# A gated delta rule on one core: products stored position by position, and some of them formed on GpSimd

## The chip, the core and the metric

The kernel is one program on 1 of the 8 cores of a Trainium2 chip. The metric is the device time of one execution in microseconds (us), median of several runs.

## What is computed

Two transformer layers over 2 x 512 tokens of width 256, each an attention and a mixture of experts, joined by modulated layer norms and residual sums. The change lies in the attention of the second layer, a gated delta rule with 16 heads, keys of 8 and values of 16 numbers:

```python
q = _l2norm(q) * SCALE; k = _l2norm(k)
def step(S, inp):                      # one token of one head
    q_t, k_t, v_t, g_t, b_t = inp
    S = S * exp(g_t)
    mem = einsum('bhk,bhkv->bhv', k_t, S)
    delta = (v_t - mem) * b_t
    S = S + einsum('bhk,bhv->bhkv', k_t, delta)
    return S, einsum('bhk,bhkv->bhv', q_t, S)
```

Its output goes through an RMS norm and a gate to the output projection. All of this is fp32.

## The kernel before, in words

Every partition holds one quarter (128 tokens, `CT`) of the tokens of one head of one batch. These are cut into `CC` = 16 chunks of `C` = 8 positions. Inside a chunk the recurrence is solved in closed form, and a scan over the 64 chunks of a sequence (`NB`) then carries the 8x16 state. Most operands are stored `(d c t)`: dimension, chunk, and the position inside the chunk innermost. A pair product is stored `(d c j)`, with the earlier position j innermost.

A sum over j, or over key dimensions, is done by TensorE: each product slice is the moving operand against the identity, and the slices add up in PSUM. An fp32 matmul stands in the trace as two MATMUL records, each of which streams all its columns. The stages, in order, with the lines of the profile:

- **Front** (VectorE, lines 1849 to 1958; GpSimd 643 to 662). Decays and betas, unit keys and queries (`unit`), the pair products k.k and q.k (`pair_products`, L1897; summed by TensorE at L1334), the rows `X24` = (16 value rows, 8 key rows) times beta (L1919, L1920), and the backward substitution (`rank_one` L1934, `less` L1939). GpSimd forms the decays `Di`, the scaled keys (L657) and the scaled queries `qa` (L661).
- **Value and matrix sums.** For each of 8 key dimensions k, VectorE multiplies all 24 rows of X24 by one row of R16 (L1970, 3072 elements). TensorE sums the 16 value rows over j, 8 slices of 256 columns (L1342). VectorE reduces the 8 key rows over j itself into the transition matrix `Msb` (L1980) and works on the query rows of the substitution between (L1934, L1939). There are three product buffers, so product k waits for TensorE's sum k-2 from the fourth on.
- **Query sums.** TensorE spreads the first two blocks of `Msb` (L1355). VectorE forms the query rows' key products `q_prod(t)` (L1995), TensorE adds them to `qa` (L1372, L1374), ScalarE copies the result to `Qp` (L917).
- **Output sums.** VectorE forms the query rows' value products `o_prod(t)` (L2002), (t+1) x 256 elements for position t; TensorE sums them (L1383), 36 slices of 256 columns. Ahead of them TensorE spreads the first half of the queries of group 0 (L1379), behind them the second half (L1387), which ScalarE copies (L936) ahead of `n_slot(2)` (L928), and the scan needs `n_slot(2)` for its ninth step.
- **Scan and states.** VectorE runs 63 steps of two products (L2020, one operand in PSUM) and two reductions (L2027). For every 8 steps (h = 0 to 7) `spread_m(h)` brings in a block of the matrix, GpSimd forms queries times states in 4 instructions (L674), TensorE sums them (L1400, 8 slices of 256 columns), and ScalarE copies them to `seqU` (L942). After every second h TensorE spreads them over the partitions and adds them to the output sums (L1409, 16 matmuls of 128 columns). `queries(g)` (L1362) brings in the queries of the next group.
- **Output.** Copies to `oT1`, norm, gate, projection, then the second mixture of experts, which starts when all of this is done.

Each engine runs its instructions in the order written; waits are on counting semaphores written out by hand. The loops of TensorE around the change, at L1381 and L1390, are

```python
for t in O_ORDER:
    pe.wait_ge(s["x_prod"], 2 * DK + O_ORDER.index(t) + 1)
    for j in range(t + 1):
        ins = pe.matmul(..., ident[:, :], o_prod(t)[:, :, :, j], ...)
...
for h in range(NHALF):
    if h + 2 < NHALF:
        spread_m(h + 2)
    if h % 2 == 0 and g + 1 < NCG:
        queries(g + 1)
    pe.wait_ge(s["state_prod"], h + 1)
```

## Time and profile before

| | before |
|---|---|
| median of 3 runs | 954.7 us (953.11 to 954.99) |
| profiled execution | 956.23 us |
| its span in the trace | 954.1 us |
| TensorE matmul busy | 862.5 us, 90% |
| VectorE busy | 538.6 us, 56% |
| GpSimd busy | 210.1 us, 22% |
| mean granted clock of TensorE | 0.951 |

The profiled execution is 2.1 us longer than its span, and 1.5 us longer than the median. Busy shares are over the whole program; the stages of the delta rule named above lie between 440 and 700 us.

### The profile page before, as it was taken

How to read it: one execution, taken by the hardware profiler on the slowest of the kernel's cores; microseconds unless marked ns; L12 is line 12 of the kernel's file. 1: busy time of each engine (PE TensorE's matmuls, PEld its weight loads, DVE VectorE, ACT ScalarE, POOL GpSimd, SP SyncE). 2: the span in 40 equal slices, each digit the busy share in tenths (PEclk: the TensorE clock that was granted, in tenths of full speed). 3: DMA queues.
4: the chain of work that ended last, by engine and by line, in shares of the span. 5: the costliest groups of instructions: out<-in, count | busy, mean ns of one | idle time of the engine just before them, and what ended most of it. 6: DMA issues, size and time to landing. Idle time of an engine off the chain costs nothing.

```text
span 954.1 us, 11526 instructions
## 1 busy us (share of the span) xinstructions
PE 862.5 (90%) x3978; PEld 588.0 (62%) x4008; DVE 538.6 (56%) x1275; ACT 253.9 (27%) x409; POOL 210.1 (22%) x189
## 2 busy tenths in 40 slices
PE   5889999879999999989869999899986799999983
PEld 4322333657777777754544475477753598999973
DVE  4787982654444444468999633387147533333426
ACT  2445775423333333335300000111121000000000
POOL 3630000212222222202200000255100243444410
PEclk9988999879999999999989999999997899999995
DMA  8763001101111111303300030000001589999944
GB/s 279 179 153 68 2 3 34 34 17 33 49 49 46 37 49 49 117 1 99 100 0 0 1 89 0 0 1 1 0 1 45 217 293 322 346 339 339 343 140 159
DMA packets 37122, 96.22 MB, mean 101 GB/s; under 512 B 4990, under 2 KB 17846, under 8 KB 36118
## 3 DMA queue, kind: packets, MB, share of 16 engines
q1 hardware_dynamic: 32982, 85.29, 27.9%
q0 software_dynamic: 3648, 9.97, 2.9%
q10 hardware_dynamic: 448, 0.39, 0.2%
q8 instruction: 26, 0.43, 0.2%
q14 instruction: 18, 0.15, 0.0%
HBM read 83.26 MB, written 13.16 MB: 101 GB/s over the span
## 4 chain that ended last, share of the span: by engine, by line
PE 78%; DVE 13%; DMA 4%; ACT 2%; issue 2%; SPq 1%; ACTq 0%; POOL 0%; DVEq 0%; POOLq 0%
PE psum L1225 15%; PE psum L1496 8%; PE psum L1506 7%; PE psum L1236 7%; PE psum L1342 6%; PE psum L1383 3%; PE psum L1409 3%; PE psum L1400 3%; PE psum L1104 3%; PE psum L1114 3%; PE psum L1125 3%; PE psum L1304 3%; PE psum L1374 2%; DVE small L1657 2%; PE psum L1314 1%
## 5 line engine op out<-in xcount | busy, mean ns | idle before, releaser
L1225 PE MATMUL psum<-xr,wr 128*128 128x512 f32 x600 | 158.9, 415 | 1.1 <-DVE arena L1806 1.1
L1225 PEld LDWEIGHTS psum<-xr,wr 128*128 128x128 f32 x600 | 116.0, 194 | 25.5 <-issue 1.4
L629 POOL TENSOR_TENSOR wr<-ring,wr 128x512 fp32r<-128x512 f32 (+1 forms) x50 | 54.5, 1109 | 196.6 <-ACT wr L797 196.6
L1657 DVE TENSOR_REDUCE small<-psum 128x1 f32<-128x512 f32 x128 | 81.0, 684 | 13.6 <-PE psum L1104 12.9
L1496 PEld LDWEIGHTS psum<-arena 128*128 128x128 f32 x700 | 83.3, 191 | 4.7 <-issue 1.5
L1496 PE MATMUL psum<-arena 128*128 128x128 f32 x700 | 84.0, 274 | 2.1 <-ACT arena L992 1.1
L1506 PE MATMUL psum<-arena 128*128 128x256 f32 x350 | 83.0, 384 | 1.9 <-DVE arena L2186 1.9
L1236 PE MATMUL psum<-hr,wr 128*128 128x512 f32 x300 | 76.2, 390 | 0.2 <-DVE hr L1744 0.2
L2175 DVE TENSOR_SCALAR arena<-psum,arena 128x256 f32<-128x256 f32 x35 | 16.9, 484 | 103.9 <-PE psum L1506 103.9
L674 POOL TENSOR_TENSOR arena<-hT,arena 128x512 f32<-128x512 f32 x32 | 36.2, 1163 | 165.1 <-ACT hT L936 140.3
L1769 DVE TENSOR_TENSOR hid<-hid,psum 128x512 f32<-128x512 f32 x50 | 34.4, 689 | 67.4 <-ACT hid L803 67.4
L776 ACT ACTIVATE arena<-psum 128x1024 f32<-128x1024 f32 x64 | 63.1, 1023 | 31.3 <-PE psum L1114 30.6
L1506 PEld LDWEIGHTS psum<-arena 128*128 128x128 f32 x350 | 64.3, 192 | 10.2 <-issue 2.3
L1342 PE MATMUL psum<-arena,ident 128*128 128x256 f32 x128 | 59.4, 642 | 9.4 <-DVE arena L1970 9.4
L1236 PEld LDWEIGHTS psum<-hr,wr 128*128 128x128 f32 x300 | 56.5, 189 | 12.4 <-issue 0.6
L691 POOL DMA_INDIRECT z_scratch<-arena x35 | 34.6, 989 | 97.7 <-DVE arena L2175 97.7
L810 ACT ACTIVATE hr<-hid 128x512 fp32r<-128x512 f32 x50 | 31.6, 632 | 90.7 <-DVE hid L1816 77.2
L1744 DVE TENSOR_TENSOR hr<-hid,hr 128x512 fp32r<-128x512 f32 x50 | 34.6, 692 | 35.5 <-ACT hr L810 35.4
L685 POOL DMA_INDIRECT arena<-h_scratch,arena x35 | 34.5, 987 | 86.0 <-DVE arena L2152 75.6
L1342 PEld LDWEIGHTS psum<-arena,ident 128*128 128x128 f32 x128 | 28.0, 219 | 40.5 <-issue 29.8
L992 ACT ACTIVATE arena<-psum 128x256 f32<-128x256 f32 x35 | 13.4, 384 | 145.0 <-PE psum L1485 145.0
L2186 DVE TENSOR_SCALAR arena<-psum,arena 128x128 f32<-128x128 f32 x175 | 48.2, 342 | 5.8 <-PE psum L1496 5.8
(360 smaller groups left out, 1276.1 us busy)
## 6 DMA issues: line engine op xcount, KB each, us to landing
arena<-in_w1u SPq DMA_DIRECT2D x35, 642.5 KB, 5.8
arena<-in_w1d SPq DMA_DIRECT2D x35, 640.0 KB, 5.3
ring<-in_w SPq DMA_DIRECT2D x25, 384.0 KB, 3.0
part_scratch<-arena SPq DMA_DIRECT2D x12, 256.0 KB, 4.2
arena<-z_scratch SPq DMA_DIRECT2D x8, 384.0 KB, 6.7
arena<-part_scratch SPq DMA_DIRECT2D x9, 256.0 KB, 7.8
qkv_scratch<-arena SPq DMA_DIRECT2D x4, 512.0 KB, 2.7
arena<-qkv_scratch SPq DMA_DIRECT2D x4, 512.0 KB, 4.0
```

The source lines that it names most:

```text
L629: pool.tensor_tensor(wr0[:, k, LO, part], ring0[:, k, part], wr0[:, k, HI, part], ALU.subtract).then_inc(s["w0_lo"], 1)
L674: ins = pool.tensor_tensor(sprod[:, h % 2, :, v, :].rearrange("p k (c t) -> p k c t", t=C), qB[g % 2][:, :, at8].rearrange("p k (c t) -> p ...
L691: pool.indirect_dma_start(z_dram, bass.IndirectOffsetOnAxis(ap=dst_i[:, r:r + 1], axis=0), yb[:, r % 3, :], None).then_inc(s[f"y_out{r % 3 ...
L776: act.activation(pexp[:, lo:lo + 2, :], psum[:, 2 + p % 2 * 2:4 + p % 2 * 2, :], ACT.Exp, scale=HD ** -0.5).then_inc(s["exp"], 1)
L1225: ins = pe.matmul(bank[2 * b + m][:, :], wr0[:, k, w, lo:lo + P], xr[:, x, f, half(b)], start=(f == 0 and (w, x) == PARTS[0]), stop=(f == ...
L1236: ins = pe.matmul(bank[4 + 2 * m + b][:, :], wr0[:, k, w, lo:lo + P], hr[:, b, x, :], start=(first and (w, x) == PARTS[0]), stop=(last and ...
L1342: ins = pe.matmul(bank[2 + k // 2][:, k % 2 * DV * CC:(k % 2 + 1) * DV * CC], ident[:, :], mn[k % 3][:, 0:DV, :].rearrange("p x (c j) -> p ...
L1496: ins = pe.matmul(bank[2 + r % 2 * 3 + k // 2][:, tile(k % 2)], wup1[:, r % 3, lo:lo + P], xgT[:, r % 2, f, :], start=(f == 0), stop=(f == ...
L1506: ins = pe.matmul(bank[1][:, 0:D], hact[:, r % 2, tile(k)], wdn1[:, r % 3, k * D:(k + 1) * D], start=(k == 0), stop=(k == NC1 - 1))
L1657: dve.tensor_reduce(nm[:, g % 2, at16:at16 + 1], full("scores", n), AX, ALU.max, negate=True).then_inc(s["bank_free"], 1)
L1744: dve.tensor_tensor(hr[:, b, LO, :], hid[:, 2 + b, :], hr[:, b, HI, :], ALU.subtract).then_inc(s[f"{name}_lo"], 1)
L2186: ins = dve.tensor_scalar(hact[:, r % 2, tile(k)], bank[2 + r % 2 * 3 + k // 2][:, tile(k % 2)], bias, 0.0, ALU.add, ALU.max)
```

## The change

The position in the chunk moves outermost and the chunk innermost in all the operands that are multiplied and summed: `(d t c)` for keys and queries, `(j x c)` for X24 and its products, `(j d c)` for the pair products, and `(g t v c)` for `seqU`. `unit` writes its result in the new order, from the old one; so do the rows of v, the decays and beta. The matmuls read slices without a stride. The reduction into `Msb` becomes three additions of halves. The eight `o_prod` move from VectorE to GpSimd, ahead of its state products. `spread_m(2)` moves from the loop over h to a place ahead of the last but one output sum. Half of the state products of the last block move from GpSimd to VectorE. Cut to what differs:

```diff
         QPROD = arena[:, 0:DK * PAIRS]
 
-        mn = [t.rearrange("p (x n) -> p x n", x=XR)
+        mn = [t.rearrange("p (j x c) -> p j x c", j=C, x=XR)
               for t in (arena[:, 0:XR * CT], arena[:, XR * CT:2 * XR * CT], KPROD[:, 0:XR * CT])]
         Nsb = arena[:, end:end + DV * CT]
...
+            return x.rearrange("p (j d c) -> p j d c", d=DV, c=CC)
 
         pa = KPROD[:, 0:2304].rearrange("p (u n v k x) -> p u n v k x", u=2, n=4, v=VV, k=DK)
         oT1 = KPROD[:, 0:DV * CT].rearrange("p (v n) -> p v n", v=DV)
         xn_flat = xn.rearrange("p t d -> p (t d)")
...
+        def turned(x, d):
+
+            return x.rearrange("p (d t c) -> p d t c", d=d, t=C)
...
 
-        X3 = X24.rearrange("p (d n) -> p d n", d=XR)
-        Xu = units(X24, XR)
-        R3 = R16.rearrange("p (d n) -> p d n", d=2 * C)
-        Ru = units(R16, 2 * C)
-        v3 = v2.rearrange("p (d n) -> p d n", d=DV)
+        Xt = X24.rearrange("p (j d c) -> p j d c", j=C, d=XR)
+        Ru = turned(R16, 2 * C)
 
         osq = hT.rearrange("p k (v n) -> p (k v) n", n=CT)
 
+        def state_product(eng, h, v):
+
+            at8 = slice(h % 2 * 64, h % 2 * 64 + 64)
+            return eng.tensor_tensor(sprod[:, h % 2, :, v, :].rearrange("p k (c t) -> p k c t", t=C),
+                                     qB[h // 2 % 2][:, :, at8].rearrange("p k (c t) -> p k c t", t=C),
+                                     Sall[:, 8 * h * VV * DK:8 * (h + 1) * VV * DK]
+                                     .rearrange("p (c v k) -> p v k c", v=VV, k=DK)[:, v]
+                                     .unsqueeze(3).broadcast_to((P, DK, 8, C)), ALU.mult)
+
         O_ORDER = (0, 1, 2, 3, 4, 5, 7, 6)
 
         def q_prod(i):
 
...
-            pool.tensor_tensor(qa.rearrange("p (d n) -> p d n", d=DK), q2.rearrange("p (d n) -> p d n", d=DK),
-                               by_dim(A0, DK), ALU.mult).then_inc(s["decays"], 1)
+            pool.tensor_tensor(qa.rearrange("p (t d c) -> p d t c", t=C, d=DK), qu,
+                               by_step(A0).unsqueeze(1).broadcast_to((P, DK, C, CC)),
+                               ALU.mult).then_inc(s["decays"], 1)
+
+            pool.wait_ge(s["x_prod"], 2 * DK)
+            pool.wait_ge(s["n_sum"], DK)
+            for t in O_ORDER:
+                if t == 6:
+                    pool.wait_ge(s["n_sum"], DK + 2)
+                pool.tensor_tensor(o_prod(t), Xt[:, 0:t + 1, 0:DV, :],
+                                   Ru[:, t, 0:t + 1, :].unsqueeze(2).broadcast_to((P, t + 1, DV, CC)),
+                                   ALU.mult).then_inc(s["out_prod"], 1)
+            pool.wait_ge(s["out_prod"], C)
 
...
                 pool.wait_ge(s["scan_hi"], 2 * (n0 + 7))
-                at8 = slice(h % 2 * 64, h % 2 * 64 + 64)
-                for v in range(VV):
-                    ins = pool.tensor_tensor(
-                        sprod[:, h % 2, :, v, :].rearrange("p k (c t) -> p k c t", t=C),
-                        qB[g % 2][:, :, at8].rearrange("p k (c t) -> p k c t", t=C),
-                        Sall[:, n0 * VV * DK:(n0 + 8) * VV * DK]
-                        .rearrange("p (c v k) -> p v k c", v=VV, k=DK)[:, v]
-                        .unsqueeze(3).broadcast_to((P, DK, 8, C)), ALU.mult)
-                ins.then_inc(s["state_prod"], 1)
+                for v in range(VV if h < NHALF - 1 else hv):
+                    ins = state_product(pool, h, v)
+                ins.then_inc(s["out_prod"], 1)
...
-                act.activation(seqU[:, :, h * 64:(h + 1) * 64],
-                               bank[5][:, h % 2 * 256:(h % 2 + 1) * 256].rearrange("p (v n) -> p v n", v=VV),
-                               ACT.Copy).then_inc(s["state_out"], 1)
+                act.activation(seqU[:, h // 2, :, :, h % 2 * 8:h % 2 * 8 + 8].rearrange("p t v c -> p v c t"),
+                               bank[5][:, h % 2 * 256:(h % 2 + 1) * 256]
+                               .rearrange("p (v c t) -> p v c t", v=VV, t=C), ACT.Copy).then_inc(s["state_out"], 1)
...
                     ins = pe.matmul(bank[2 + k // 2][:, k % 2 * DV * CC:(k % 2 + 1) * DV * CC], ident[:, :],
-                                    mn[k % 3][:, 0:DV, :].rearrange("p x (c j) -> p (x c) j", j=C)[:, :, j],
+                                    mn[k % 3][:, j, 0:DV, :].rearrange("p x c -> p (x c)"),
                                     start=(j == 0), stop=(j == C - 1), skip_group_check=True)
                 ins.then_inc(s["n_sum"], 1)
...
             for t in range(C):
                 pe.wait_ge(s["x_prod"], DK + t + 1)
                 to = bank[4 + t // 4][:, t % 4 * CT:(t % 4 + 1) * CT]
-                pe.matmul(to, ident[:, :], units(qa, DK)[:, :, :, t], start=True, stop=False, skip_group_check=True)
+                pe.matmul(to, ident[:, :], qa[:, t * CT:(t + 1) * CT], start=True, stop=False, skip_group_check=True)
                 for j in range(t + 1):
-                    ins = pe.matmul(to, ident[:, :], q_prod(t)[:, :, :, j], start=False, stop=(j == t),
+                    ins = pe.matmul(to, ident[:, :], q_prod(t)[:, j].rearrange("p x c -> p (x c)"), start=False, stop=(j == t),
                                     skip_group_check=True)
                 if t % 4 == 3:
                     ins.then_inc(s["n_sum"], 1)
             pe.wait_ge(s["qp_in"], 2)
             pe.matmul(bank[4][:, :], selg[:, 0, :], Qp[:, 0:4 * CT], start=True, stop=True).then_inc(s["queries"], 1)
             for t in O_ORDER:
-                pe.wait_ge(s["x_prod"], 2 * DK + O_ORDER.index(t) + 1)
+                if t == O_ORDER[-2]:
+                    spread_m(2)
+                pe.wait_ge(s["out_prod"], O_ORDER.index(t) + 1)
                 for j in range(t + 1):
                     ins = pe.matmul(bank[t // 2][:, t % 2 * 256:(t % 2 + 1) * 256], ident[:, :],
-                                    o_prod(t)[:, :, :, j],
+                                    o_prod(t)[:, j].rearrange("p x c -> p (x c)"),
                                     start=(j == 0 and t in O_ORDER[::2]), stop=False, skip_group_check=True)
...
             for h in range(NHALF):
                 g = h // 2
-                if h + 2 < NHALF:
+                if 0 < h < NHALF - 2:
                     spread_m(h + 2)
                 if h % 2 == 0 and g + 1 < NCG:
                     queries(g + 1)
-                pe.wait_ge(s["state_prod"], h + 1)
+                pe.wait_ge(s["out_prod"], C + (h + 1 if h < NHALF - 1 else NHALF + 1))
                 if h:
                     pe.wait_ge(s["state_out"], h)
...
-                            seqU[:, :, g * CT:(g + 1) * CT].rearrange("p v (c t) -> p t v c", t=C)[:, 2 * n:2 * n + 2],
+                            seqU[:, g, 2 * n:2 * n + 2].rearrange("p t v c -> p (t v c)"),
...
-            ch.link(dve.tensor_scalar(g_(0), ab2[:, 0, :], cols[:, DLT + 1:DLT + 2], None, ALU.add))
+            ch.link(dve.tensor_scalar(by_step(g_(0)), from_tokens(ab2[:, 0, :]), cols[:, DLT + 1:DLT + 2], None, ALU.add))
...
-            def unit(n, t):
-
-                t3 = t.rearrange("p (d n) -> p d n", d=DK)
+            def unit(n, t, to):
+
                 dve.wait_ge(s["d_act"], n + 7)
                 ch.link(dve.reciprocal(g_(8 + n), g_(8 + n)))
                 if n:
                     ch.link(dve.tensor_scalar(g_(9), g_(9), DK ** -0.5, None, ALU.mult))
-                dve.tensor_tensor(t3, t3, by_dim(g_(8 + n), DK), ALU.mult).then_inc(s["unit"], 1)
-
-            unit(0, k2)
+                dve.tensor_tensor(to, t.rearrange("p (d c t) -> p d t c", d=DK, t=C),
+                                  by_step(g_(8 + n)).unsqueeze(1).broadcast_to((P, DK, C, CC)),
+                                  ALU.mult).then_inc(s["unit"], 1)
+
+            unit(0, k2, ku)
...
                     for i in part:
-                        ins = dve.tensor_tensor(blocks(prod, i), ku[:, :, :, 0:i + 1],
-                                                left[:, :, :, i].unsqueeze(3).broadcast_to((P, DK, CC, i + 1)),
+                        ins = dve.tensor_tensor(blocks(prod, i), ku[:, :, 0:i + 1, :],
+                                                left[:, :, i, :].unsqueeze(2).broadcast_to((P, DK, i + 1, CC)),
                                                 ALU.mult)
...
-            t0, t1 = g_(0), g_(1)
-            first = [x.rearrange("p (c t) -> p c t", t=C)[:, :, 0] for x in (t0, t1, dec)]
-            dve.tensor_copy(t0, dec)
+            t0, t1, t2 = g_(0), g_(1), g_(7)
+            first = [x.rearrange("p (c t) -> p c t", t=C)[:, :, 0] for x in (t0, t1)]
+            dve.tensor_copy(from_tokens(t0), dec3)
             ch.link(dve.memset(t1, 0.0))
             dve.memset(first[0], 0.0)
-            ch.link(dve.tensor_copy(first[1], first[2]))
-            dve.tensor_tensor_scan(A0, t0, t1, 0.0, ALU.mult, ALU.add).then_inc(s["blocks"], 1)
-            unit(1, q2)
+            ch.link(dve.tensor_copy(first[1], dec3[:, 0, :]))
+            ch.link(dve.tensor_tensor_scan(t2, t0, t1, 0.0, ALU.mult, ALU.add))
+            dve.tensor_copy(by_step(A0), from_tokens(t2)).then_inc(s["blocks"], 1)
+            unit(1, q2, qu)
...
-            dve.tensor_tensor(X3[:, DV:XR, :], k2.rearrange("p (d n) -> p d n", d=DK), by_dim(t0, DK), ALU.mult)
-            x_rows = ch.mark(dve.tensor_tensor(X3[:, 0:DV, :], v3, by_dim(beta, DV), ALU.mult))
+            dve.tensor_tensor(Xt[:, :, DV:XR, :].rearrange("p j d c -> p d j c"), ku,
+                              by_step(t0).unsqueeze(1).broadcast_to((P, DK, C, CC)), ALU.mult)
+            x_rows = ch.mark(dve.tensor_tensor(Xt[:, :, 0:DV, :],
+                                               v2.rearrange("p (d c t) -> p t d c", d=DV, t=C),
+                                               by_step(beta).unsqueeze(2).broadcast_to((P, C, DV, CC)), ALU.mult))
...
-                prod = Sall[:, at:at + n * CC * i].rearrange("p (r c j) -> p r c j", r=n, c=CC)
-                return prod, dve.tensor_tensor(prod, Ru[:, part, :, i].unsqueeze(3).broadcast_to((P, n, CC, i)),
-                                               pair_row(Lr, i)[:, :, 0:i].unsqueeze(1).broadcast_to((P, n, CC, i)),
+                prod = Sall[:, at:at + n * CC * i].rearrange("p (r j c) -> p r j c", r=n, c=CC)
+                return prod, dve.tensor_tensor(prod, Ru[:, part, i, :].unsqueeze(2).broadcast_to((P, n, i, CC)),
+                                               pair_row(Lr, i)[:, 0:i, :].unsqueeze(1).broadcast_to((P, n, i, CC)),
                                                ALU.mult)
 
             def less(i, part, prod):
-                return dve.tensor_tensor(Ru[:, part, :, 0:i], Ru[:, part, :, 0:i], prod, ALU.subtract)
+                return dve.tensor_tensor(Ru[:, part, 0:i, :], Ru[:, part, 0:i, :], prod, ALU.subtract)
...
-                ins = dve.tensor_tensor(Ru[:, i, :, 0:i + 1],
+                ins = dve.tensor_tensor(Ru[:, i, 0:i + 1, :],
                                         bank[7 if i >= C - 2 else 6][:, lo:lo + CC * (i + 1)]
-                                        .rearrange("p (c j) -> p c j", c=CC), pair_row(Di, i), ALU.mult)
+                                        .rearrange("p (j c) -> p j c", c=CC), pair_row(Di, i), ALU.mult)
...
             for k in range(DK):
                 if k >= 3:
                     dve.wait_ge(s["n_sum"], k - 2)
-                made = dve.tensor_tensor(mn[k % 3], X3, R3[:, C + k, :].unsqueeze(1).broadcast_to((P, XR, CT)),
-                                         ALU.mult)
-                made.then_inc(s["x_prod"], 1)
+                prods = mn[k % 3]
+                dve.tensor_tensor(prods, Xt, Ru[:, C + k].unsqueeze(2).broadcast_to((P, C, XR, CC)),
+                                  ALU.mult).then_inc(s["x_prod"], 1)
 
                 i = C - 1 - k
                 if i:
-                    ch.need(turned)
+                    ch.need(solved)
                     prod, ins = rank_one(i, slice(i, C), 1024)
                     formed = ch.mark(ins)
                 dve.wait_ge(s["x_prod"], k + 1)
-                ins = dve.tensor_reduce(M3[:, k], units(mn[k % 3].rearrange("p x n -> p (x n)"), XR)[:, DV:XR],
-                                        AX, ALU.add)
-                reduced = ch.mark(ins)
+                ch.link(dve.tensor_tensor(prods[:, 0:4, DV:XR, :], prods[:, 0:4, DV:XR, :], prods[:, 4:8, DV:XR, :],
+                                          ALU.add))
+                halved = ch.mark(dve.tensor_tensor(prods[:, 0:2, DV:XR, :], prods[:, 0:2, DV:XR, :],
+                                                   prods[:, 2:4, DV:XR, :], ALU.add))
                 if i:
                     ch.need(formed)
-                    turned = ch.mark(less(i, slice(i, C), prod))
-                ch.need(reduced)
+                    solved = ch.mark(less(i, slice(i, C), prod))
+                ch.need(halved)
+                summed = ch.mark(dve.tensor_tensor(M3[:, k], prods[:, 0, DV:XR, :], prods[:, 1, DV:XR, :], ALU.add))
+            ch.need(summed)
             diag = Msb.rearrange("p (c e) -> p c e", c=CC)[:, :, 0:DK * DK:DK + 1]
-            dve.tensor_tensor(diag, diag, A0.rearrange("p (c t) -> p c t", t=C)[:, :, C - 1].unsqueeze(2)
+            dve.tensor_tensor(diag, diag, by_step(A0)[:, C - 1, :].unsqueeze(2)
                               .broadcast_to((P, CC, DK)), ALU.add).then_inc(s["m_done"], 1)
             dve.memset(Sall[:, 0:VV * DK], 0.0).then_inc(s["blocks"], 1)
 
-            ch.need(turned)
+            ch.need(solved)
...
             for t in range(C):
-                dve.tensor_tensor(q_prod(t), Xu[:, DV:XR, :, 0:t + 1],
-                                  Ru[:, t, :, 0:t + 1].unsqueeze(1).broadcast_to((P, DK, CC, t + 1)),
+                dve.tensor_tensor(q_prod(t), Xt[:, 0:t + 1, DV:XR, :],
+                                  Ru[:, t, 0:t + 1, :].unsqueeze(2).broadcast_to((P, t + 1, DK, CC)),
                                   ALU.mult).then_inc(s["x_prod"], 1)
-            dve.wait_ge(s["n_sum"], DK)
-            for t in O_ORDER:
-                if t == 6:
-                    dve.wait_ge(s["n_sum"], DK + 2)
-                dve.tensor_tensor(o_prod(t), Xu[:, 0:DV, :, 0:t + 1],
-                                  Ru[:, t, :, 0:t + 1].unsqueeze(1).broadcast_to((P, DV, CC, t + 1)),
-                                  ALU.mult).then_inc(s["x_prod"], 1)
-
...
             dve.wait_ge(s["scan_lo"], 2 * (NB - 1))
             dve.wait_ge(s["scan_hi"], 2 * (NB - 1))
+            dve.wait_ge(s["qB"], 2 * NCG)
+            dve.wait_ge(s["state_sum"], NHALF - 2)
+            dve.wait_ge(s["out_prod"], C + NHALF - 1)
+            for v in range(hv, VV):
+                ins = state_product(dve, NHALF - 1, v)
+            ins.then_inc(s["out_prod"], 1)
```

Here `turned(x, d)` is `(d t c)`, `from_tokens(x)` reads `(c t)` as t, c, and `by_step(x)` is `(t c)`.

## Rows read from the trace of the kernel before

**Rows 1.** Chain of waits, 440 to 700 us: start, duration, engine and line, pieces.

```profile
496.07 59.38 PE psum L1342 x128
...
557.18 0.46 PE psum L1372 x2
557.64 0.22 PE psum L1374 x2
...
560.74 1.81 PE psum L1374 x8
...
572.69 3.74 PE psum L1374 x16
...
577.61 2.08 PE psum L1379 x2
579.69 31.21 PE psum L1383 x72
...
639.04 3.45 PE psum L1400 x16
...
647.28 7.69 PE psum L1409 x32
```

**Rows 2.** Timeline of VectorE: start, duration, line, shape, idle before.

```profile
470.44 7.13 DVE L1897 TENSOR_TENSOR arena<-arena 128x1024 f32<-128x1024 f32 x8 [0.71 <-DMA arena<-qkv_scratch]
...
492.66 3.36 DVE L1970 TENSOR_TENSOR arena<-arena 128x3072 f32<-128x3072 f32 x1
...
500.97 1.21 DVE L1980 TENSOR_REDUCE arena<-arena 128x128 f32<-128x1024 f32 x1
502.10 0.35 DVE L1939 TENSOR_TENSOR arena<-arena 128x192 f32<-128x192 f32 x1
502.37 3.35 DVE L1970 TENSOR_TENSOR arena<-arena 128x3072 f32<-128x3072 f32 x1
...
507.40 3.35 DVE L1970 TENSOR_TENSOR arena<-arena 128x3072 f32<-128x3072 f32 x1
...
526.07 3.36 DVE L1970 TENSOR_TENSOR arena<-arena 128x3072 f32<-128x3072 f32 x1 [2.35 <-PE psum L1342]
...
613.18 0.47 DVE L2020 TENSOR_TENSOR arena<-arena,psum 128x128 f32<-128x128 f32 x2
...
613.99 0.48 DVE L2020 TENSOR_TENSOR arena<-arena,psum 128x128 f32<-128x128 f32 x2
```

**Rows 3.** Groups by shape on VectorE, 540 to 547 us (mean ns last).

```profile
L1995 DVE TENSOR_TENSOR arena<-arena 128x512 f32<-128x512 f32 x1 | 0.7, 684 | 0.0
...
L1995 DVE TENSOR_TENSOR arena<-arena 128x128 f32<-128x128 f32 x1 | 0.4, 387 | 2.3 <-PE psum L1342 2.3
```

**Rows 4.** Groups by shape on VectorE, 481.9 to 492.6 us.

```profile
L1939 DVE TENSOR_TENSOR arena<-arena 128x128 f32<-128x128 f32 x2 | 0.5, 284 | 0.0
```

**Rows 5.** Groups by shape on VectorE, 457.5 to 466.4 us.

```profile
L1897 DVE TENSOR_TENSOR arena<-arena 128x1024 f32<-128x1024 f32 x1 | 3.3, 3253 | 0.0
L1887 DVE TENSOR_TENSOR arena<-arena,rt 128x1024 f32<-128x1024 f32 x1 | 1.2, 1225 | 0.0
```

**Rows 6.** Timeline of GpSimd, 440 to 700 us.

```profile
457.68 3.32 POOL L657 TENSOR_TENSOR arena<-arena 128x1024 f32<-128x1024 f32 x1 [4.54 <-DVE arena L1887]
...
618.29 4.51 POOL L674 TENSOR_TENSOR arena<-hT,arena 128x512 f32<-128x512 f32 x4 [1.33 <-DVE arena L2027]
```

**Rows 7.** Groups by shape on ScalarE, 440 to 700 us.

```profile
L912 ACT ACTIVATE arena<-psum 128x256 f32<-128x256 f32 x8 | 4.4, 664 | 81.3 <-PE psum L1342 81.3
...
L942 ACT ACTIVATE hid<-psum 128x256 f32<-128x256 f32 x8 | 3.1, 384 | 31.7 <-PE psum L1400 31.7
```

**Rows 8.** Stretches: length; PE, PEld, DVE, ACT, POOL busy; clock; DMA share, GB/s.

```profile
464.00:466.00 2.00, 1.11 (x5) 1.11 (x6) 2.00 (x4) 0.84 (x2) 0.00 (x0) 0.60 0.77 294
470.00:472.00 2.00, 1.12 (x5) 1.06 (x6) 1.56 (x1) 0.83 (x2) 2.00 (x1) 1.00 0.14 44
...
577.00:578.00 1.00, 0.39 (x1) 0.39 (x2) 1.00 (x1) 1.00 (x3) 0.00 (x0) 0.52 0.00 0
```

34 lines of the change are left out of this document (19 added, 15 removed).

## The prediction

> **What bounds the kernel now.** The page's busy shares don't say what the delta rule waits for, so I read the chain of waits between 440 and 700 us first. From 496.07 on it is nearly all TensorE: the value sums (59.38 us), the query sums (to 576.43), the output sums (31.21 us), then eight state sums of 3.45 us and four spreads of 7.69 us [rows 1]. Next come the widths. A state sum reads 256 adjacent columns and takes 3.45/16 = 0.216 us a record. A value sum, also 256 columns against the same identity, reads every eighth word and takes 59.38/128 = 0.464 us; an output sum takes 31.21/72 = 0.433 us. The query sums show that the stride is the cause. All are 128 columns, and the stride in words is t+1: 0.22/2 = 0.11 us at t=0, 1.81/8 = 0.226 at t=3, 3.74/16 = 0.234 at t=7 [rows 1]. The spread (stride 8, 128 columns) takes 7.69/32 = 0.240. So from a stride of four words a record costs twice as much.
> The Trainium skill (SBUF — State Buffer, the note on cachelines in its DMA port part) says that SBUF is read in lines of 16 bytes and that an access pattern which leaves the line at every element is slower; the step to 0.226 us at 16 bytes agrees.
>
> VectorE is the second engine. In the value stage its round takes 5.03 us (502.37 to 507.40) against TensorE's 7.4, and from the sixth product on it waits about 2.35 us a round [rows 2]. Before 492.66 VectorE has no wait but one of 0.71 us for v's transfer, and sets the pace.
>
> **Front (VectorE, adds).** `unit` twice and the rows of v now read or turn every eighth word: 1024 + 1024 + 2048 elements. The price per element: a product of 128 with both inputs at stride 8 took 387 ns [rows 3], one of 128 with adjacent runs 284 ns [rows 4], so 0.8 ns more. Upper bound 4096 x 0.8 = 3.3 us; the lower is 0, since only one input of the three is strided. I take 0.65 ns, 2.7 us, near the upper end, plus 0.6 us for the short strided operations on 128 numbers and the new copy of A0. The wait for v's transfer, 0.71 us [rows 2], disappears behind that; the few products of one position that were strided gain 0.2 us. Net +2.4, rounded to +2.9 for semaphores (bounds 0 and +4).
> The Trainium skill (Vector Engine (DVE) Microarchitecture Reference, the part on the SBUF access granule) gives 2.5 ns a column where both sources or the output step by 24 words, against 1.05 adjacent; by that the three would cost an estimated 6 us and the front +6.
>
> **Value sums.** TensorE's share falls from 7.4 to 16 x 0.216 = 3.46 us a key dimension, so VectorE becomes the bound. Its reduction step (500.97 to 502.10, 1.13 us [rows 2]) gives way to additions of 512, 256 and 128 elements. The first is waited for: 0.684 + 0.03. The second and third overlap with neighbours, 0.34 and 0.2: between the 684 ns of 512 elements and the 284 of 128 [rows 3, 4], less some 0.08 of overlap. That is 1.25, +0.12 a round: 5.15 us. Eight rounds: 7 x 5.15 + 3.36 for the last product + 3.46 for its sum = 42.9 us, against 555.46 - 492.66 = 62.8 now. **-19.9 us.** The waits on the product buffers go.
>
> **Query sums.** Then 1.72 us of spreads as now, and 72 + 16 records at 0.115 us = 10.1 us against 576.43 - 557.18 = 19.25. **-9.1 us.** VectorE's eight `q_prod` (36 x 128 elements, about 6 us at the 684 ns of 512 [rows 3]) begin 2 us before TensorE needs them, so they stay ahead.
>
> **Output sums.** The handover (ScalarE's copy, L1379) stays at 3.3 us. TensorE then needs 72 x 0.216 = 15.55 us plus 0.86 for `spread_m(2)`, against 31.21: **-14.8 us.** The products move to GpSimd: 36 x 256 = 9216 elements. Its price: 4 x 512 elements in 4.51 us is 2.2 ns an element; L657, with a wait for VectorE in it, is 3.32/1024 = 3.24 at most [rows 6]. A plain lower bound is 1.04, VectorE's own. I take 2.2, since L674 multiplies by a broadcast operand too: 20.7 us. GpSimd can start when the last `q_prod` is done, about 10 us before TensorE reaches the output sums. Then t=7 is ready 17 us after that start, and TensorE comes to it after 10 + 42 x 0.216 + 0.86 = 20; t=6 is ready at 20.7, and TensorE comes at 23.4. Hidden, with 3 us to spare. If this cover were gone, every further 1 ns an element would cost 9.2 us. VectorE's share for them, some 10 us at the 3.36 us of 3072 elements [rows 2], also goes, but it lay beside TensorE and is worth nothing by itself. It lets the scan begin right after the query sums: eight steps of 0.81 us [rows 2], about 5 us ahead of TensorE's reaching `spread_m(2)`, which waits for them. That wait has `o_prod(7)` and (6) behind it on TensorE. The ninth step still waits for `n_slot(2)`, behind the second half of the queries, so the scan gains no more than the chain: up to there +2.9 -19.9 -9.1 -14.8 = **-40.9 us**.
>
> **Scan and states.** From there on TensorE stays the chain. The spreads shrink to 32 x 0.111 = 3.55 us: 4 x (7.69 - 3.55) = -16.5 us. ScalarE's copy to `seqU` writes with a stride; its like, L912, takes 664 ns against 384 [rows 7]: +0.28, five times on the chain, +1.4. Moving `spread_m(2)` gives nothing back here, as TensorE had a wait for `queries(1)` in that place. Two blocks of h then cost TensorE 2 x 3.45 + 3.55 + 1.7 for two block spreads + some 3 for queries and copies = 15.2 us, VectorE 16 x 0.81 = 13.0, GpSimd 9.0, so neither of these binds. The last half-product on VectorE shortens GpSimd's last 4.5 us, but TensorE is then still at the block before: nothing. **-15.1 us.** The rest of the program (output stage, experts) is a copy of now, later work starting earlier by the same amount.
>
> **The sum.** -40.9 - 15.1 = -56.0 us. Profiled execution: 956.2 - 56.0 = 900.2. The median shown is 1.5 lower, 954.7 - 56.0 = 898.7, so **899 us**.
>
> **Rivals.**
> *A, TensorE's clock in the gaps.* In the value stage TensorE would work 3.46 of 5.15 us. After a wait of 1.18 us its next record ran at 0.52 of the clock (1.2 GHz level), and L1379 took 1.04 us a record; 464 to 466 shows 0.60 with 1.11 us busy of 2, but 470 to 472 shows 1.00 with 1.12 busy [rows 1, 8]. So it can fall and need not. At half clock a round costs TensorE 6.9 us, 8 x 6.9 = 55.3 instead of 42.9: +12.4, **911 us**. TensorE would then be busy without a gap, as it is in the value stage now, whose records are of the fast kind (0.464, not 0.93), so this is an upper end. Chance 0.14.
> The Trainium skill (TensorE: Matmul & The Clock Gate, part 1) has the throttled state as the default and activity as what releases it; that is this rival.
> *B, GpSimd binds the output sums.* At 3.24 ns an element it needs 29.9 us; with 3.0 us of sums for t=6 behind it, the stage ends 5.5 us later: **904 us**. For it: L657. Against: L657 began beside a VectorE product of 1.22 us, and that engine's next product took 3.25 us instead of 1.2 [rows 5, 6], so the two held each other up; the scan's products, with one operand in PSUM, ran at their usual pace beside L674. Chance 0.11.
> The Trainium skill (SBUF — State Buffer, who interferes with whom) says the same: two SBUF inputs on VectorE contend with GpSimd's reads; that the scan's do not rests on this.
> *C, slower.* The same mechanism as A, but from the value stage to the end of the states: with gaps in every stage the clock stays at 1.2 GHz. The records double: 55.3 + 3.4 + 20.2 + 3.3 + 31.1 + 3.5 + 6 + 55.4 + 28.4 + about 24 for spreads, queries and copies = 231 us from 492.66 to 690.4, which now takes 198: **about 991 us**. It decides once more than some 60% of this work runs at half clock. Against: from output sums on TensorE is to be busy 90% of the time. Chance 0.02.
> *D, the change doesn't do it.* If records of adjacent slices kept 0.43 us, nothing but the front and the copies would change: +4, **959 us**. Rows 1 have both widths on both kinds of access. Chance 0.01.
>
> **How the numbers follow.** Forecast 0.72 with its own range 893 to 905 (front 0 to +4, gap costs, the handover at full clock -1). A measurement of this kernel can tell about 0.2% (1.9 us) from no change. Range: 891 to 912 takes in A and B, and leaves out C, D and a little. Faster 0.96, same 0.01, slower 0.03.
>
> **What would show it.** L1342's records 0.216 us apart, with VectorE's next product following without a wait; L1374 and L1409 0.11; the output sums about 16 us with GpSimd's products 2.2 ns an element and done before TensorE asks; the scan's first eight steps before `spread_m(2)`, the rest waiting for `n_slot(2)`; `unit` at about 1.9 us. It would be wrong if TensorE waits for GpSimd in the output sums, if its clock is at 0.5 for more than the first rounds, or if the strided writes of `unit` and ScalarE cost several times their bounds.

## The result, and the profile after

| | before | after |
|---|---|---|
| median of 4 runs, same chip | 953.9 us (952.62 to 954.99) | 897.92 us (897.22 to 898.6) |
| profiled execution | 956.23 us | 898.13 us |
| its span in the trace | 954.1 us | 895.7 us |
| TensorE matmul busy | 862.5 us | 790.4 us, 88% |
| VectorE busy | 538.6 us | 534.0 us, 60% |
| GpSimd busy | 210.1 us | 229.9 us, 26% |
| mean granted clock | 0.951 | 0.951 |

The ratio of the medians is 0.9414 (95%: 0.9397 to 0.943): 56.0 us less. The profiled executions differ by 58.1 us. The surplus lies behind the delta rule: from L2063 (L2033 in before) to the end the program took 263.7 us in the trace of before and 260.7 in that of after. Of these 3.0 us, 1.3 came of an expert's weights (`in_w1u`) that arrived late once in that profile of before, and 1.7 of TensorE's clock, which stood at half there over the last sums of the experts (3.67 + 4.08 us against 2.41 + 3.62). Steps are therefore judged by stages.

The chain of waits of after, start and duration in us, engine, line and pieces, is to be read against [rows 1]:

```profile
495.42 3.36 DVE arena L2000
...
534.34 3.72 PE psum L1364 x16
...
547.81 1.80 PE psum L1396 x16
...
550.79 1.12 PE psum L1401 x2
551.91 9.07 PE psum L1407 x42
560.98 0.86 PE psum L1377 x2
561.84 6.47 PE psum L1407 x30
568.31 0.87 PE psum L1411 x2
574.12 2.08 PE psum L1384 x2
576.19 5.17 PE psum L1424 x16
...
586.54 3.84 PE psum L1433 x32
...
602.62 3.84 PE psum L1433 x32
...
631.14 3.85 PE psum L1433 x32
```

All four kinds of record that had a stride take half the time now: the output sums (L1407) (9.07 + 6.47)/72 = 0.216 us against 0.433, the query sums 1.80/16 = 0.113 against 0.234, the spreads (L1433) 3.84/32 = 0.120 against 0.240, the value sums (L1364) 3.72/16 = 0.233 against 0.464. These have left the chain but for the last 16, and VectorE's product (L2000) stands there instead.

The timeline of VectorE (DVE) in after, in the front and for one round of the value stage (compare [rows 2]):

```profile
456.02 2.02 DVE L1910 TENSOR_TENSOR arena<-arena,rt 128x1024 f32<-128x1024 f32 x1
458.07 1.22 DVE L1916 TENSOR_TENSOR arena<-arena,rt 128x1024 f32<-128x1024 f32 x1
...
480.27 3.88 DVE L1947 TENSOR_TENSOR arena<-arena,rt 128x2048 f32<-128x2048 f32 x1
...
505.42 3.35 DVE L2000 TENSOR_TENSOR arena<-arena 128x3072 f32<-128x3072 f32 x1
508.69 0.39 DVE L1963 TENSOR_TENSOR arena<-arena 128x240 f32<-128x240 f32 x1
509.00 0.68 DVE L2009 TENSOR_TENSOR arena<-arena 128x512 f32<-128x512 f32 x1
509.72 0.43 DVE L2011 TENSOR_TENSOR arena<-arena 128x256 f32<-128x256 f32 x1
510.06 0.40 DVE L1968 TENSOR_TENSOR arena<-arena 128x240 f32<-128x240 f32 x1
510.38 0.37 DVE L2017 TENSOR_TENSOR arena<-arena 128x128 f32<-128x128 f32 x1
510.59 3.35 DVE L2000 TENSOR_TENSOR arena<-arena 128x3072 f32<-128x3072 f32 x1
```

A round is 510.59 - 505.42 = 5.17 us, and no row has a wait in brackets: VectorE never stops. The timeline of GpSimd (POOL), whose last column is the idle time before and what ended it:

```profile
458.18 3.32 POOL L674 TENSOR_TENSOR arena<-arena 128x1024 f32<-128x1024 f32 x1 [5.43 <-DVE arena L1910]
...
541.74 20.71 POOL L687 TENSOR_TENSOR arena<-arena 128x256 f32<-128x256 f32 x8 [67.01 <-DVE arena L2027]
...
620.36 3.19 POOL L330 TENSOR_TENSOR arena<-hT,arena 128x512 f32<-128x512 f32 x2 [2.21 <-DVE arena L2051]
```

L687 is the moved `o_prod`: 9216 elements in 20.71 us, done at 562.45, while TensorE works through L1407 without a break until 568.31. Last, TensorE's clock, in stretches of after (length; PE, PEld, DVE, ACT, POOL busy; clock; DMA share, GB/s):

```profile
490.00:505.00 15.00, 6.16 (x16) 4.99 (x17) 14.90 (x37) 0.00 (x0) 0.00 (x0) 0.52 0.00 0
505.00:538.00 33.00, 26.03 (x115) 21.01 (x114) 32.69 (x44) 3.27 (x6) 0.00 (x0) 1.00 0.00 1
...
574.00:576.00 2.00, 1.89 (x3) 0.85 (x4) 2.00 (x11) 0.06 (x1) 0.74 (x2) 0.50 0.00 0
```

The value stage begins at half clock, as TensorE had waited 14.07 us for the first product, and from 505 on it has the full clock although TensorE is busy for 26 of 33 us. At 574, behind a wait of 3.13 us, the clock is at half again.

### The profile page after: what moved, and what is told of

It is laid out like the page before. It is cut to its first block, busy times and chain, and to the rows that moved or that the text cites. A ratio compares the mean times of both kernels' runs of the same rounds, so it can differ in the third digit from the quotient of the medians.

```text
span 895.7 us, 11541 instructions
## 1 busy us (share of the span) xinstructions
PE 790.4 (88%) x3978; PEld 562.5 (63%) x4008; DVE 534.0 (60%) x1286; ACT 254.8 (28%) x409; POOL 229.9 (26%) x195
## 4 chain that ended last, share of the span: by engine, by line
PE 74%; DVE 18%; DMA 3%; ACT 2%; issue 1%; SPq 1%; ACTq 0%; POOL 0%; DVEq 0%; POOLq 0%
PE psum L1247 16%; PE psum L1520 9%; PE psum L1530 8%; PE psum L1258 7%; PE psum L1424 3%; PE psum L1147 3%; PE psum L1136 3%; DVE arena L2000 3%; PE psum L1326 3%; PE psum L1126 3%; DVE small L1681 2%; PE psum L1407 2%; PE psum L1433 2%; PE psum L1336 2%; PE psum L1356 1%
## 5 line engine op out<-in xcount | busy, mean ns | idle before, releaser
L1364 PE MATMUL psum<-arena,ident 128*128 128x256 f32 x128 | 32.3, 410 | 21.0 <-DVE arena L2000 21.0
L1126 PE MATMUL psum<-arena 96*128 96x512 bf16 x128 | 45.8, 392 | 3.2 <-DVE small L1681 2.3
L825 ACT ACTIVATE hid<-psum 128x512 f32<-128x512 f32 x50 | 29.9, 599 | 51.4 <-PE psum L1247 51.4
```

The source lines that it names most:

```text
L1126: pe.matmul(to, Qt[t][0:KR, j, b * S + qt * P:b * S + (qt + 1) * P], Kt[t][0:KR, j, half(b)], start=True, stop=True).then_inc(s["bank_full ...
```

## The experiments

Three measures are used. The medians stand beside runs of before on the same chip. The time up to the value stage differs between profiles of the same work (the first 3072-element product starts at 491.91 us in e7 and at 497.42 in e11, with the same code ahead of it), so I also take the **distance** from the end of the last value sum (L1364; 538.06 in after) to the end of the last spread (L1433; 631.14 + 3.85 = 634.99): 96.93 us in after. The third measure is the length of the **value stage**, from the first 3072-element product to that same last sum: 538.06 - 495.42 = 42.64 us. The runs e2, e3 and e4 have two executions each, the others four to six.

| kernel | median, us | ratio to before (95%) | distance, us |
|---|---|---|---|
| after | 897.92 | 0.9414 (0.9397 to 0.943) | 96.93 |
| e11, after once more | 899.9 | 0.9431 (0.9404 to 0.9458) | 96.96 |
| e1, `o_prod` on VectorE | 896.4 | 0.9419 (0.9387 to 0.9451) | 97.09 |
| e2, `o_prod` twice | 914.73 | 0.9601 (0.9567 to 0.9634) | 114.96 |
| e3, strided value sums | 912.73 | 0.958 (0.9539 to 0.962) | stage 58.95 |
| e4, `seqU` as before | 913.55 | 0.9588 (0.9546 to 0.963) | states +14.0 |
| e5, `spread_m(2)` late | 895.77 | 0.94 (0.937 to 0.943) | 94.19 |
| e6, queries early | 893.91 | 0.9376 (0.9341 to 0.9411) | 90.86 |
| e7, reduction | 903.61 | 0.9493 (0.9461 to 0.9524) | stage 46.56 |
| e8, TensorE kept at work | 897.08 | 0.941 (0.9382 to 0.9439) | 95.05 |
| e9, all queries early | 888.12 | 0.9305 (0.9279 to 0.9331) | 86.17 |
| e10, last block on GpSimd | 898.08 | 0.9413 (0.9388 to 0.9438) | 97.26 |
| e12, GpSimd beside VectorE | 903.44 | 0.9481 (0.9454 to 0.9508) | 96.60, stage 46.95 |

**e11, the kernel after once more**, with no edit, as the measure for what e9, e10 and e12 showed on their chip.

> The changed kernel, unchanged, on the same chip as the three runs beside it, so that their times can be set against it: 898 us by every theory.

Its stage is 42.65 us (497.42 to 540.07) and its distance 96.96, those of after within 0.03 us, while its median is 2 us higher. So differences of 1 us between medians say nothing here. The distance has a scatter of its own: the state sums of h=0 begin at half clock, and as the clock rises sooner or later they take 5.17 us in after, 4.18 in e3, 4.22 in e2, 4.86 in e12, 5.33 in e1 and 5.50 in e10. A difference of distances below 1 us is read with these numbers beside it.

**e3, the value sums with a stride again.** TensorE alone gets the old access back, and nothing changes for VectorE:

```diff
-  mn[k % 3][:, j, 0:DV, :].rearrange("p x c -> p (x c)"),
+  mn[k % 3][:, j, 0:DV, :].rearrange("p x c -> p c x"),
```

> The changed kernel with one thing different: the value sums' 256 columns are read in the order chunk, row instead of row, chunk, from the same products (a stride of 16 words instead of adjacent ones), and ScalarE's copy undoes the order. My theory: the stride alone makes a record take 0.46 us instead of 0.22, TensorE's share of a round is 7.4 us and it is the bound again: the stage is 19 to 21 us longer (918 us), with VectorE waiting 2.3 us a round. Rival D: the stride is not the cause: no change.

The value stage took 58.95 us, 16.3 more than in after. The chain of waits of e3:

```profile
498.02 55.54 PE psum L1364 x128
```

55.54/128 = 0.434 us a record, without a break. VectorE waited for it only ahead of its seventh and eighth products, 0.60 and 1.80 us, where 2.3 us a round had been expected. The direction is as expected and the size a little lower, since a record with a stride of 16 words took 0.434 us where the one with a stride of 8 took 0.464 [rows 1]. So the stride alone, not the order of the products, made the value sums bind.

**e7, the reduction in place of three additions.** The change had three VectorE instructions for one; this goes back to one.

```diff
-  ch.link(dve.tensor_tensor(... prods[:, 0:4] + prods[:, 4:8] ...))
-  halved = ch.mark(dve.tensor_tensor(... [:, 0:2] + [:, 2:4] ...))
...
-  summed = ch.mark(dve.tensor_tensor(M3[:, k], ... [:, 0] + [:, 1] ...))
+  summed = ch.mark(dve.tensor_reduce(M3[:, k],
+                   prods[:, :, DV:XR, :].rearrange("p j x c -> p x c j"), AX, ALU.add))
```

> The changed kernel with the three additions of halves replaced by one reduction over j, now with a stride of 384 words. My theory: a reduction of 1024 elements with such a stride takes 1.9 to 2.0 us (L1901, 2004 ns) against 1.3 for the three, so a round of VectorE, which is the bound, grows by 0.6 us, seven times: 4 us slower (902 us). Rival: TensorE is the bound in this stage after all: no change.

The timeline of VectorE in e7:

```profile
500.89 1.93 DVE L2009 TENSOR_REDUCE arena<-arena 128x128 f32<-128x1024 f32 x1
...
502.99 3.36 DVE L2000 TENSOR_TENSOR arena<-arena 128x3072 f32<-128x3072 f32 x1
```

The reduction of 1024 numbers takes 1.93 us where j is outermost and took 1.21 where it was innermost [rows 2]. The stage is 46.56 us, +3.9. So VectorE binds: a round that is 0.55 us longer (39.51/7 = 5.64 against 35.68/7 = 5.10), seven times, costs 3.9 us, and that is what the halving additions are worth.

**e2, every `o_prod` formed twice on GpSimd**, which asks what GpSimd's cover is worth.

```diff
+  for again in range(2):
+      ins = pool.tensor_tensor(o_prod(t), ...)
```

> The changed kernel with every o_prod formed twice on GpSimd (the same numbers twice). My theory (rival B of the prediction turned into a run): GpSimd's stage goes from 20.7 to 41.4 us, ends at 583 us, and the last 14 records of sums come behind it: the output sums end near 586.3 instead of 568.3, 18 us slower (916 us). If GpSimd were on the chain already, it would cost 20.7; if its cover were larger than I read, less than 15.

The timeline of GpSimd in e2:

```profile
542.04 42.23 POOL L688 TENSOR_TENSOR arena<-arena 128x256 f32<-128x256 f32 x16 [67.01 <-DVE arena L2031]
```

42.23 us for twice the elements, the output sums ended 19.0 us later behind the value sums than in after, and the distance grew by 18.0 (the state sums of h=0 took 4.22 us instead of 5.17). GpSimd's price is 2.29 ns an element, and its cover is gone well before twice its work. It starts 3.7 us behind the last value sum; with 42.2 us of products and 3.3 of sums for t=6 behind them that makes the 49.26 us to the end of the output sums (538.36 to 587.62), which in after took 30.25.

**e1, the `o_prod` back on VectorE**, ahead of the scan; GpSimd starts with its state products.

```diff
-  pool.tensor_tensor(o_prod(t), ...)
+  dve.tensor_tensor(o_prod(t), ...)
```

> The changed kernel with the eight o_prod put back on VectorE, in the new layout. My theory: the move to GpSimd is worth nothing by itself. VectorE is free from 541.7 us on and would finish them near 552; the scan then starts 2 us later than in the changed kernel (549.7), its first eight steps end near 559, and TensorE comes to spread_m(2) at 561. Expected: the changed kernel's time within 0.2% (898 us). Rival: the early start of the scan carries part of the gain; then 2 to 10 us slower than the changed kernel.

The timeline of VectorE in e1:

```profile
541.15 10.24 DVE L2027 TENSOR_TENSOR arena<-arena 128x256 f32<-128x256 f32 x8
551.30 0.48 DVE L2044 TENSOR_TENSOR arena<-arena,psum 128x128 f32<-128x128 f32 x2
```

The products take 10.24 us there, the scan (L2044) starts at 551.30, and the distance is 97.09, +0.16, which is what the state sums of h=0 took more. The half of the change that goes by its name to GpSimd brings nothing by itself: the first eight steps of the scan are early with it or without it, and the ninth waits for `n_slot(2)` either way.

**e5, `spread_m(2)` back in the loop over h.**

```diff
-  if t == O_ORDER[-2]:
-      spread_m(2)
...
-  if 0 < h < NHALF - 2:
+  if h < NHALF - 2:
```

> The changed kernel with spread_m(2) back in the loop over h. My theory: TensorE's output sums get 0.86 us shorter, and at h = 0 the spread lies in TensorE's wait for the queries of group 1, so the time falls by 0.9 us (897 us). Rival: the early spread is needed by the scan; then the time rises by 0.9 us or more.

The distance fell by 2.74 us. 0.86 of it is the spread itself, gone from the output sums: in the late place it fills the 0.69 us in which TensorE waited for the first half of the queries of group 1. The other 1.9 came as a surprise, and the stretches of e5 behind the output sums show it (the wait of 3.13 us lies at 567 to 570):

```profile
568.00:570.00 2.00, 0.00 (x0) 0.00 (x0) 2.00 (x11) 0.86 (x2) 2.00 (x3) 1.00 0.00 0
570.00:572.00 2.00, 1.98 (x7) 1.40 (x8) 2.00 (x12) 0.60 (x1) 0.73 (x2) 1.00 0.00 0
```

The timelines of TensorE around this wait, first before, then after, then e5:

```profile
612.45 1.12 PE L1362 MATMUL psum<-xn,arena 128*128 128x512 f32 x2
616.71 1.13 PE L1362 MATMUL psum<-xn,arena 128*128 128x512 f32 x2 [3.14 <-ACT hT L936]
```

```profile
569.86 1.12 PE L1384 MATMUL psum<-xn,arena 128*128 128x512 f32 x2 [0.69 <-ACT hT L958]
574.12 2.08 PE L1384 MATMUL psum<-xn,arena 128*128 128x512 f32 x2 [3.13 <-ACT hT L958]
```

```profile
564.92 1.02 PE L1377 MATMUL psum<-arena 128*128 128x512 f32 x2
565.77 1.12 PE L1384 MATMUL psum<-xn,arena 128*128 128x512 f32 x2
570.02 1.12 PE L1384 MATMUL psum<-xn,arena 128*128 128x512 f32 x2 [3.13 <-ACT hT L958]
```

The clock stays at 1.00 where in after it fell to 0.50, behind an equally long wait. The second half of the queries (L1384) took 1.12 us instead of 2.08, the state sums of h=0 3.47 (571.14 to 574.61) instead of 5.17; then those of h=1 waited 0.71 us for GpSimd, which is late next. The place of the spread goes with it in part. In all nine traces with the early spread and this wait left empty (after, e1 to e4, e7, e10 to e12), TensorE waited 0.69 us, worked on the first half of the queries and waited 3.13 us, and the second half then took 2.05 to 2.08 us. With the late spread the 0.69 us are gone, and the second half took 1.13 us in before and 1.12 in e5. But in before the clock fell 1.2 us later: its state sums of h=0 took 5.14 us. Only e5 kept it, and the profiled execution of e5 is the fastest of its six (891.14 us, mean clock 0.960; the others took 895.54 to 898.5 us at 0.949 to 0.952). So 0.86 us of the gain belong to the edit, and the other 1.9 may belong to that one execution; the medians on this chip, 895.77 us against 896.4 of e1, say no more.

**e8, TensorE kept at work in that wait**: 20 matmuls of 256 columns into an unused half of a bank.

```diff
+  if g == 1 and x == 1:
+      for _ in range(20):
+          pe.matmul(bank[5][:, 256:512], identb[:, :], sel0[:, 0:256], ...)
   pe.wait_ge(s["qB"], 2 * g + x)
```

> The changed kernel with 20 bf16 matmuls of 256 columns, into an unused half bank, in TensorE's 3.1 us wait for the queries of group 1. They compute nothing that is used. My theory: the clock that falls to 0.5 at 573 us stays at 1.0, so L1384's second half takes 1.13 us instead of 2.08 and the first state sum 3.45 instead of 5.17: 2.7 us less (895 us). Rival: the clock falls anyway, or the state sum then waits for GpSimd: no change.

The clock stayed at 1.00 and the distance fell by 1.88 us, less than expected, because of the same 0.70 us of waiting for GpSimd at h=1. The spread is early here, as in the nine traces in which the clock was at half behind the empty wait, so this speaks for the matmuls; it rests on one profile, and the median (897.08 against 896.4 of e1 on the same chip) shows no gain. The price of the lower clock in this place is the same in e5 and e8: some 1.9 us.

**e6, the second half of the first queries among the output sums.** After the output sums TensorE sends the second half of the queries (L1411), and ScalarE's copy of them, `n_slot(2)`, eight steps of the scan and GpSimd's first products come one after another from there. The edit moves the matmul to t=2.

```diff
+  if t == 2:
+      pe.wait_ge(s["qB"], 1)
+      pe.matmul(bank[4][:, :], selg[:, 0, :], Qp[:, 4 * CT:8 * CT], ...)
   if t == O_ORDER[-2]:
       spread_m(2)
...
-  pe.wait_ge(s["qB"], 1)
-  pe.matmul(bank[4][:, :], selg[:, 0, :], Qp[:, 4 * CT:8 * CT], ...)
```

> The changed kernel with the second half of the queries of group 0 (TensorE's L1411) moved from behind the output sums to between output sums 1 and 2. My theory: it is what holds back ScalarE's n_slot(2), with it the scan's ninth step, the queries of group 1 and GpSimd's first state products. With it early, the first state sum starts about 4 us sooner after the output sums instead of 7.0 us behind them and finds the clock up: 6 us less (892 us; bounds 4 and 8). Rival: the scan is the bound anyway, or another wait takes its place: no change.

The chain of waits of e6:

```profile
562.65 6.48 PE psum L1411 x30
569.13 0.87 PE psum L1384 x2
...
570.67 1.12 PE psum L1384 x2
571.80 3.45 PE psum L1425 x16
```

The wait of 3.13 us is gone, with it the low clock, and the distance is 6.07 us shorter. The medians fell by less (893.91), with an interval that overlaps that of after (e1 on the same chip: 896.4), so the gain of e6 rests on the traces.

**e9, all queries sent ahead**, on top of e6: `queries(1)` goes among the output sums too, and those of group g+2 ahead of and behind the spread of group g.

```diff
+  if t == 5:
+      queries(1, 0)
...
+  queries(1, 1)
   for h in range(NHALF):
-      if h % 2 == 0 and g + 1 < NCG:
-          queries(g + 1)
...
+      if g + 2 < NCG:
+          queries(g + 2, 0)
       pe.wait_ge(s["state_out"], h + 1)
...
+      if g + 2 < NCG:
+          queries(g + 2, 1)
```

> e6_query_early, and in addition TensorE's two halves of every later group of queries are set apart, so that ScalarE's copy of the first lies beside sums: the first half of group 1 ahead of output sum 5, its second half behind the output sums; the first half of group g+2 between the second state sum and the spread of group g, its second half behind that spread. My theory: TensorE is the chain from the output sums to the end of the states, so what it waits for is time: 1.8 us before the first state sum, 0.74 us in two more groups, 0.7 us of ScalarE's copy of the states in two, and some 1 us of the part of the matmuls that a wait exposes: 5 us less than e6_query_early, 11 less than the changed kernel (887 us; bounds 8 and 12). Rival: VectorE's scan, 13.0 us for two blocks against TensorE's 14.6 then, becomes the bound at the start and gives back more than half of it.

The chain of waits of e9:

```profile
571.90 3.45 PE psum L1425 x16
575.36 0.86 PE psum L1377 x2
576.22 3.63 PE psum L1425 x16
579.85 0.86 PE psum L1383 x2
580.70 3.68 PE psum L1436 x32
...
586.10 3.45 PE psum L1425 x16
```

There is no ScalarE piece between L1425 and L1436 and none ahead of L1383: the copies lie beside TensorE's work. Two blocks take 586.10 - 571.90 = 14.20 us, in after 602.62 - 586.54 = 16.08. With 888.12 us, 11.8 less than after on the same chip and with an interval clear of it, this version beats both kernels. The distance is 10.76 shorter.

**e4, `seqU` in the old order**, so that L1433 reads with a stride of 8 words and ScalarE writes without one.

```diff
-  seqU[:, h // 2, :, :, h % 2 * 8:h % 2 * 8 + 8].rearrange("p t v c -> p v c t")
+  seqU[:, :, h * 64:(h + 1) * 64]
...
-  seqU[:, g, 2 * n:2 * n + 2].rearrange("p t v c -> p (t v c)")
+  seqU[:, :, g * CT:(g + 1) * CT].rearrange("p v (c t) -> p t v c", t=C)[:, 2 * n:2 * n + 2]
```

> The changed kernel with seqU in its old layout: TensorE's spread of the states reads with a stride of 8 words, ScalarE's copy writes adjacent words. My theory: 3.84 us become 7.7 four times, the copy 0.61 becomes 0.39 five times on the chain: +14.3 us (912 us). Rival: the scan or GpSimd is so close behind that less than half of it shows.

The chain of waits of e4:

```profile
603.60 0.39 ACT hid L964
...
623.56 7.69 PE psum L1433 x32
```

Both sizes of before are back: 7.69 and 0.39. From the first state sum to the end of the last spread it is 72.78 us (574.35 to 647.13), against 576.19 to 634.99 = 58.80 in after: +14.0, where 4 x 3.85 - 5 x 0.22 gives 14.3. The second state sum of a pair, which waits for ScalarE's copy of the first, took 3.47 us as in before, and 3.65 in after: that takes back another 0.5, and the state sums of h=0 took 0.2 more (5.39).

**e10, all of the last block on GpSimd**, as before the change.

```diff
-  for v in range(VV if h < NHALF - 1 else hv):
+  for v in range(VV):
```

> The changed kernel with all four state products of the last block on GpSimd again. My theory: no change, since TensorE comes to them at 626.7 us and GpSimd would end near 624.9. Rival: the half on VectorE is on the chain; then 1.3 us or more slower.

898.08 us, distance 97.26; the +0.33 is that of the state sums of h=0 (5.50 us against 5.17). GpSimd took 4.49 us for its four products here and 3.19 for its two in after, as VectorE's own two ran beside them; either way TensorE is still at the block before. So this part of the change is worth nothing either.

**e12, two products of GpSimd beside VectorE in the value stage.** They read two inputs of 1024 from SBUF into an unused tile.

```diff
+  for n in range(2):
+      pool.wait_ge(s["x_prod"], 2 * n + 2)
+      pool.tensor_tensor(hid[...], X24[:, 0:1024], X24[:, 1024:2048], ALU.mult)
```

> The changed kernel with two extra products of 1024 elements on GpSimd in the value stage, where it has nothing to do (their result is not used), one behind VectorE's second product, one behind its fourth. My theory: GpSimd and a VectorE product with both operands in SBUF can't run side by side, as at L674 and L1922, so each costs VectorE's chain its own 2.2 us: the stage is 4.4 us longer. Rival: that pair collides for another reason and the engines share: less than 1 us.

The timelines of e12, GpSimd's row first, then VectorE's:

```profile
501.52 2.38 POOL L684 TENSOR_TENSOR hid<-arena 128x1024 f32<-128x1024 f32 x1 [29.04 <-DVE arena L2004]
```

```profile
496.63 0.68 DVE L2013 TENSOR_TENSOR arena<-arena 128x512 f32<-128x512 f32 x1
...
501.62 2.84 DVE L2013 TENSOR_TENSOR arena<-arena 128x512 f32<-128x512 f32 x1
...
514.09 2.84 DVE L2013 TENSOR_TENSOR arena<-arena 128x512 f32<-128x512 f32 x1
```

The addition that comes 0.1 us behind GpSimd's start takes 2.84 us instead of 0.68, twice, and the stage is 46.95 us, 4.3 longer = 2 x 2.16. So VectorE does not slow down in proportion; it stands until GpSimd, which began first, is done, while GpSimd nearly keeps its pace (2.38 and 2.47 us for 1024 elements, where 2.25 ns an element gives 2.30). Behind the value stage, where `o_prod` lies, the same engine's 20.71 us cost nothing.
The Trainium skill (SBUF — State Buffer, the part on who interferes with whom) calls the shared port an exclusive lock held for a whole instruction, with the loser fully blocked; e12 agrees.

## Why the prediction was right

The forecast of 899.0 us lies 1.1 us from the median of 897.92, inside its own range (893 to 905). The medians differ by the 56.0 us of the sum (the 1.1 is the median of before, 953.9 now and 954.7 then, and rounding). That they agree to 0.1 us is luck, as the same kernel once more gave 899.9; and not each term came as forecast:

| step | forecast, us | measured, us |
|---|---|---|
| front | +2.9 | 495.42 - 492.66 = +2.8 |
| value sums | 42.9, -19.9 | 42.64, -20.2 |
| query sums | -9.1 | -9.4 |
| handover L1401 | 0 | -1.0 |
| output sums | -14.8 | 568.31 - 551.91 = 16.40, -14.8 |
| to the end of the second half of the queries | -40.9 | -42.6 |
| to the first state sums | 0 | +0.95 |
| state sums and spreads | -15.1 | 72.54 to 58.80, -13.7 |
| all of the delta rule, to the copy L2063 | -56.0 | -55.4 |

The start of the first product wanders by up to 5.5 us between traces, so the row of the front is firmer when taken from the first `unit` on: 492.66 - 456.31 = 36.35 us in before, and 39.40, 39.41 and 39.42 in after, e5 and e11. That is +3.05, and the delta rule as a whole, taken so, -55.1.

- **Stride.** That records of adjacent columns cost half is shown from both sides: by after, where four kinds of them halve, and by e3 and e4, where two of them double again and take 16.3 and 14.0 us with them.
- **Value sums.** The round is 4.9 to 5.2 us, 5.10 in the mean, and has VectorE as its bound, as forecast with 5.15. e7 shows that by adding to VectorE alone.
- **Front.** The price of a stride at one input was taken as 0.65 ns an element and is (2.02 - 1.23)/1024 = 0.77 [rows 5 have the 1.23], and (3.88 - 2.29)/2048 = 0.78; the three operations cost 3.2 us instead of 2.7, and the rest of the front less than forecast (the sum of its own terms was 2.4, raised to 2.9 for semaphores), so that the total was right with two errors against each other. The prediction also overlooked a wait of 0.87 us of VectorE for ScalarE ahead of 443.74; it is 0.77 in after and changes nothing. The upper bound of 0.8 was the better value: one strided input costs about as much as two did in the product of 128 elements that it came from.
The Trainium skill (Vector Engine (DVE) Microarchitecture Reference, the part on the SBUF access granule) gives 2.5 ns a column where both sources or the output step by 24 words; here, where one source steps by 8 words, it was 2.02/1.024 = 1.97.
- **Query rows on GpSimd.** 20.71 us against 20.7, hidden. But e1 shows that the move is neither needed nor worth anything: it is cover against cover.
- **`spread_m(2)`.** "Gives nothing back" holds: 0.86 us more in the output sums, and e5 shows none of it returned. This part of the change is a small loss, and its edit is the first to undo. The forecast has no term for the lower clock that goes with the early spread, next.
- **Handover and the wait behind the output sums.** The forecast left both as they were. The clock decided both: L1401 took 1.12 us at full clock where it (then L1379) had taken 2.08 [rows 1], behind the same wait of 1.18 us, and 1.12 or 1.13 in all thirteen traces of the new layout. L1384 took 2.08 where it had taken 1.13, behind the early spread, as in all nine such traces. They cancel, by chance, and why either went its way stays open.
- **States.** The step "the spreads shrink to 32 x 0.111 = 3.55 us" was mis-sized: each measured 3.84. The whole of 4 x 0.29 = 1.2 us is missing in the sum. ScalarE's copy cost 5 x 0.22 = 1.1 where 1.4 was forecast, but it also holds back the second state sum of three pairs (3.65 us against 3.47), 0.5 that the forecast lacks: -15.4 + 1.1 + 0.5 = -13.8, against -13.7 measured.
- **Rival A** (half clock in the value stage, 911 us) did not happen: the clock was at half only in the first 6 us of sums, and TensorE had made that up by the end of the third product, before VectorE needed it. In e7 it fell once more in this stage (519 to 522 us, 0.51), and there too VectorE did not wait. The rival took 0.464 us a record as a sign of full clock; it is none, since records with this stride take as long at half clock (see the last section). **Rival B** (GpSimd binds at 3.24 ns, 904 us) did not happen: the price was 2.25 ns. By its own terms it comes to 905 us, as 29.9 + 3.0 lies 6.5 us behind 10 + 16.4, not 5.5. The 3.24 ns holds a wait: L674 began at 458.18 beside VectorE's L1916, which ended at 459.29, and took 3.32 us; from there to its end it is 2.21 us for 1024 elements, the usual price. Beside `o_prod` VectorE ran only the scan, whose products have one input in PSUM; e12 shows what two inputs in SBUF cost VectorE. **C** and **D** are excluded by the result.
